# Output projection of attention computed feature-major and transposed back, its input passes one unit earlier

## The reference, cut to what matters

```python
h = _L0_tok_ref(x, ...)                                   # (16, 512, 128)
h = h + _L0_attn_ref(_layernorm(h), W_qkv, b_qkv, W_out, b_out)
h = h + _L0_ffn_ref(_layernorm(h), router_w, router_b, Wi, Wh, b, Wo, bo)
# at the end of _L0_attn_ref:
out = jnp.concatenate([out_wtok, out_fea], axis=1)
return out @ W_out + b_out
```

## Time and profile before

| | us |
|---|---|
| median of 3 runs | 1867.98 |
| lowest, highest | 1867.66, 1868.47 |
| the profiled execution | 1867.89 |
| its span, first to last instruction | 1866.0 |
| TensorE busy | 1740.3 |
| Vector busy | 1542.1 |
| ScalarE busy | 997.0 |

### The profile page before, as it was taken

The page is one execution under the profiler, slowest core; times in us unless marked ns, Lnnn a source line. Parts: engine busy times, 40 slices in busy tenths (PEclk is TensorE's granted clock), DMA queues, the critical chain, the costliest instruction groups (busy, mean ns, idle before and its releaser), DMA issues.

```text
span 1866.0 us, 25899 instructions
## 1 busy us (share of the span) xinstructions
PE 1740.3 (93%) x9898; PEld 852.3 (46%) x9898; DVE 1542.1 (83%) x2417; ACT 997.0 (53%) x1114; POOL 38.0 (2%) x42
## 2 busy tenths in 40 slices
PE   4447899999999999999999999999999999999998
PEld 2223444444444444544444444444444444444443
DVE  2649897988889888898988889898888988889865
ACT  4225645646465554646546464565646556464544
POOL 0000000000000000000000000000000000000000
PEclk9768999999999999999999999999999999999999
DMA  3123221313123131221323223131322314232121
GB/s 117 21 36 83 64 64 52 74 41 82 47 53 74 44 79 42 64 68 40 74 56 70 43 63 64 49 77 39 78 53 52 75 45 71 49 63 68 45 63 37
DMA packets 203905, 110.95 MB, mean 59 GB/s; under 512 B 125642, under 2 KB 184892, under 8 KB 203782
## 3 DMA queue, kind: packets, MB, share of 16 engines
q1 hardware_dynamic: 203782, 109.30, 25.8%
HBM read 89.84 MB, written 4.74 MB: 51 GB/s over the span
## 4 chain that ended last, share of the span: by engine, by line
PE 61%; DVE 26%; issue 7%; ACT 4%; DMA 1%; SPq 1%; POOL 0%; DVEq 0%; ACTq 0%
PE gates L528 45%; PE yp L534 4%; DVE tmp L1024 3%; DVE tmp L1003 2%; DVE xm L996 2%; DVE Hs L1008 2%; DVE C L1028 2%; DVE tmp L1018 2%; DVE tmp L1039 2%; ACT tmp L677 2%; PE FB L488 2%; PE FA L469 2%; PE FB L487 2%; PE FA L454 2%; DVE z L1043 1%
## 5 line engine op out<-in xcount | busy, mean ns | idle before, releaser
L670 ACT ACTIVATE tmp<-gates,bias_sb 128x1024 f32<-128x1024 f32 x504 | 559.7, 1111 | 571.4 <-PE gates L528 570.1
L528 PE MATMUL gates<-xm,wi_sb 128*128 128x512 f16 x3024 | 759.1, 389 | 14.2 <-DVE xm L996 9.5
L528 PE MATMUL gates<-Hs,wh_sb 128*128 128x512 f16 x2880 | 708.1, 382 | 0.0
L528 PEld LDWEIGHTS gates<-xm,wi_sb 128*128 128x128 f16 x3024 | 294.5, 100 | 410.9 <-issue 117.0
L528 PEld LDWEIGHTS gates<-Hs,wh_sb 128*128 128x128 f16 x2880 | 284.8, 99 | 349.1 <-issue 16.3
L677 ACT ACTIVATE tmp<-C 128x1024 f32<-128x1024 f32 x128 | 135.2, 1056 | 149.6 <-DVE C L1028 145.7
L1003 DVE SCALAR_TENSOR_TENSOR tmp<-tmp 128x1024 f32<-128x1024 f32 x128 | 156.5, 1223 | 58.6 <-ACT tmp L677 56.7
L1018 DVE SCALAR_TENSOR_TENSOR tmp<-tmp 128x1024 f32<-128x1024 f32 x120 | 145.2, 1210 | 64.3 <-ACT tmp L670 64.3
L1024 DVE SCALAR_TENSOR_TENSOR tmp<-tmp,C 128x1024 f32<-128x1024 f32 x120 | 145.7, 1214 | 39.4 <-ACT tmp L670 38.8
L996 DVE TENSOR_TENSOR xm<-xs,masks 128x2048 f16<-128x2048 f16 x128 | 155.7, 1217 | 11.8 <-DMA masks<-mask_scratch 11.8
L1008 DVE SCALAR_TENSOR_TENSOR Hs<-tmp,Hs 128x1024 f16<-128x1024 f32 x120 | 146.7, 1222 | 16.3 <-ACT Hs L681 16.3
(11 more groups left out here) (155 smaller groups left out, 1231.0 us busy)
## 6 DMA issues: line engine op xcount, KB each, us to landing
masks<-mask_scratch SPq DMA_DIRECT2D x128, 256.0 KB, 5.2
roww<-mw_scratch SPq DMA_DIRECT2D x128, 256.0 KB, 3.5
rowk<-mask_scratch SPq DMA_DIRECT2D x128, 128.0 KB, 2.9
diag<-pr SPq DMA_DIRECT2D x64, 112.0 KB, 3.2
diag<-vwin SPq DMA_DIRECT2D x64, 112.0 KB, 3.2
out_dram<-h SPq DMA_DIRECT2D x16, 256.0 KB, 2.2
C<-in_wi SPq DMA_DIRECT2D x1, 2048.0 KB, 10.4
C<-in_wh SPq DMA_DIRECT2D x1, 2048.0 KB, 15.1
```

What stands on the lines that cost most here:

```text
L528: last = mm(gates[:, slot, k * SEQ:(k + 1) * SEQ], w, v, start=(i < K), stop=(i >= len(seq) - K))
L670: A(tmp[:, gate_at(gate, e), :], gates[:, (n - 1) % 2, :], ACT.Tanh, bias=bias_sb[:, e, gate:gate + 1], scale=UNSCALE).then_inc(s_tanh, 1)
```

## The change

The projection is computed feature-major: `wout_sb` is the stationary operand, the whole of `attn` (512 columns) the moving one, and the result, features by tokens, lies in `FA[:, 1, :]`. ScalarE reads it, adds the bias (now one value per partition) and writes `xnT`; TensorE transposes the four tiles back into `FB`, where the token-major result lay before. The matmul is in unit 16 on TensorE, ScalarE's pass in unit 16, the transposes in unit 17. Vector's four passes L914 move from unit 16 to unit 15, behind f_part of unit 14. `ones1` and its memset go, and the bias is loaded as a column.

```diff
--- before.py
+++ after.py
@@ -54,12 +54,12 @@
 
 
     SP_AT = dict(ids=-8, qbd=1, vz=5, rows=25, wrow=28)
-    PE_AT = dict(emb=-5, xT=-2, qkv=-1, summary=2, window=4, feature=10, values=15, proj=17, x2T=20,
+    PE_AT = dict(emb=-5, xT=-2, qkv=-1, summary=2, window=4, feature=10, values=15, proj=16, projT=17, x2T=20,
                  logits=21, maskT=25)
-    ACT_AT = dict(h=-5, xT=-2, qkv=-1, split=0, summary=4, window=7, pr_hi=11, feature=12, x2T=20,
+    ACT_AT = dict(h=-5, xT=-2, qkv=-1, split=0, summary=4, window=7, pr_hi=11, feature=12, proj=16, x2T=20,
                   choice=22, maskT=25)
     DVE_AT = dict(onehot=-6, moments=-4, xn=-3, pw=0, q_lo=0, kv_lo=1, v_win=2, w_max=3, s_max=5, s_sub=6, w_sum=7,
-                  w_out=8, s_sum=9, s_norm=10, f_max=11, p_lo=12, p_T=13, f_sum=14, f_part=14, attn=16,
+                  w_out=8, s_sum=9, s_norm=10, f_max=11, p_lo=12, p_T=13, f_sum=14, f_part=14, attn=15,
                   moments2=18, xn2=19, x_lo=21, choice1=22, choice2=22, weights=23)
     EARLY = 8
     MASKS_AT = 26
@@ -148,8 +148,7 @@
         rw_sb = sb("rw_sb", [P, E])
         rb_sb = sb("rb_sb", [P, E])
         bo_sb = sb("bo_sb", [P, D])
-        bout_sb = sb("bout_sb", [1, D])
-        ones1 = sb("ones1", [1, P])
+        bout_sb = sb("bout_sb", [P, 1])
         ident = sb("ident", [P, P])
         identb = sb("identb", [P, P], bf16)
         hones = sb("hones", [P, P])
@@ -245,7 +244,7 @@
 
         names = """ids enc onehot emb hsb bnst bnag veps rstd xn xnTp xnT qp kp vp q k v qbd vwin vz
             pw sw mw dw ew rw iw ow owr ow_c pf sf mf df ef rf if_ uf S mS dS eS rS iS prT O of0 of1
-            khi vhi qhi qlo klo vlo pn phi plo cf attn proj h2 bnst2 bnag2 veps2 rstd2 xn2 x2p xhi x32 xlo lgp lg m1 eq1 ix1 im1 k1 l2 m2
+            khi vhi qhi qlo klo vlo pn phi plo cf attn projT projS proj h2 bnst2 bnag2 veps2 rstd2 xn2 x2p xhi x32 xlo lgp lg m1 eq1 ix1 im1 k1 l2 m2
             eq2 ix2 im2 k2 dd ed sd w0 w1 wa wb wt mwc mwp mrow wT mout wout ybo"""
         S = {n: sem("f_" + n) for n in names.split()}
 
@@ -279,10 +278,13 @@
         def row(ap):
             return ap.rearrange("(a n) -> a n", a=1)
 
+        def col(ap):
+            return ap.rearrange("(n a) -> n a", a=1)
+
         consts = [
             (wqkv_sb[:, :], w_qkv), (bqkv_sb[:, :], b_qkv), (wout_sb[:, :], w_out),
             (rw_sb[:, :], router_w), (rb_sb[:, :], row(router_b).to_broadcast([P, E])), (bo_sb[WT0:WT0 + E, :], bo),
-            (bout_sb[:, :], row(b_out)), (ident[:, :], ident_dram), (hones[:, :], head_ones), (band_sb[:, :], band),
+            (bout_sb[:, :], col(b_out)), (ident[:, :], ident_dram), (hones[:, :], head_ones), (band_sb[:, :], band),
             (par_sb[:, :], parity), (m8_sb[:, :], expert_m8), (vcol[:, :], vocab_col),
             (bias_sb[:, :, :], b_lstm),
             (rows[0:ENC0 + NFR, :], frame_rows), (table[0:ENC0 + NFR, :], emb_table),
@@ -483,9 +485,11 @@
                     last.then_inc(S["O"], 1)
                 if t == PE_AT["proj"]:
                     pe.wait_ge(S["attn"], b1)
+                    mm(FA[:, 1, :], wout_sb[:, :], attn[:, :], start=True, stop=True).then_inc(S["projT"], 1)
+                if t == PE_AT["projT"]:
+                    pe.wait_ge(S["projS"], b1)
                     for i in range(TILES):
-                        mm(FB[:, i * D:(i + 1) * D], attn[:, i * P:(i + 1) * P], wout_sb[:, :], start=True, stop=False)
-                        last = mm(FB[:, i * D:(i + 1) * D], ones1[:, :], bout_sb[:, :], start=False, stop=True)
+                        last = nc.tensor.transpose(FB[:, i * D:(i + 1) * D], xnT[:, i * P:(i + 1) * P], ident[:, :])
                     last.then_inc(S["proj"], 1)
                 if t == PE_AT["x2T"]:
                     pe.wait_ge(S["xn2"], b1)
@@ -564,7 +568,7 @@
 
             pe.wait_ge(s_const, 16 * len(consts))
             pe.wait_ge(s_zero, 1)
-            pe.wait_ge(s_prep, 4)
+            pe.wait_ge(s_prep, 3)
             for t in range(-EARLY, NG * E):
                 front(t, 0)
             pe.wait_ge(s_wlo, 7)
@@ -602,7 +606,7 @@
                     act.wait_ge(S["xnTp"], b1)
                     A(xnT[:, :], FB[:, :], ACT.Copy).then_inc(S["xnT"], 1)
                 if t == ACT_AT["qkv"]:
-                    act.wait_ge(s_prep, 4)
+                    act.wait_ge(s_prep, 3)
                     act.wait_ge(S["qp"], b1)
                     if not is_zero(b):
                         act.wait_ge(S["S"], b)
@@ -639,6 +643,9 @@
                 if t == ACT_AT["feature"]:
                     act.wait_ge(S["df"], b1)
                     A(ew[:, 0:TF], prod[:, 0:TF], ACT.Exp).then_inc(S["ef"], 1)
+                if t == ACT_AT["proj"]:
+                    act.wait_ge(S["projT"], b1)
+                    A(xnT[:, :], FA[:, 1, :], ACT.Identity, bias=bout_sb[:, 0:1]).then_inc(S["projS"], 1)
                 if t == ACT_AT["x2T"]:
                     act.wait_ge(S["x2p"], b1)
                     A(x32[:, :], FB[:, :], ACT.Copy).then_inc(S["x32"], 1)
@@ -746,7 +753,6 @@
                     dve.wait_ge(s_dft_hi, 1)
                     STT(out=dft16[:, LO, :], in0=dft_sb, scalar=V_SCALE, in1=dft16[:, HI, :],
                         op0=ALU.mult, op1=ALU.subtract).then_inc(s_dft_lo, 1)
-            V.memset(ones1[:, :], 1.0).then_inc(s_prep, 1)
             dve.wait_ge(s_const, 16 * len(consts))
             V.tensor_copy(identb[:, :], ident[:, :]).then_inc(s_prep, 1)
             V.tensor_copy(bandb[:, :], band_sb[:, :]).then_inc(s_prep, 1)
```

## The result

The changed kernel takes 1821.03 us (median of 4 runs, 1818.52 to 1822.79) against 1868.22 us beside it. The ratio is 0.9744, interval [0.9728, 0.9761]: faster by 2.6%. The profiled execution has a span of 1821.0 us, 45.0 less than before.

A forecast was written before the change was run, and what follows sets the result against it. TensorE, busy 109.55 of 110.90 us per step, was taken as the bound; fourteen steps gaining 3.1 us (43.6) plus 2 and 1.5 for the first two fronts, in all 47, took 1867.9 to 1821 us, range 1809 to 1833.

The forecast's parts named there:

- The moved wait: TensorE ahead of the projection in unit 16: wait on Vector's passes not removed, 1.7 us instead of 1.4.
- Projection and weight load: TensorE, unit 16: one 512-column float32 matmul, 0.86 us, plus 0.2 us for a weight load that waits with it.
- the case for 1818: Weight load ahead of the new matmul is pulled ahead and its 0.2 us vanish: sum 3 us better.
- Tanh 17 late: ScalarE's tanh 17 begins at 1053.1, behind the later gates 17; Vector waits 1.5 us for it ahead of L1018.
- Wait for xn2: TensorE ahead of L493, unit 20: a second new wait, 0.6 us, and 0.15 us of weight load.
- ScalarE's pass: 512-wide activation adding the bias, unit 16, ahead of tanh 17: 588 ns, costing nothing on the path.
- Per step: Gates 17 to L493 takes 15.21 us against 18.33: gain 3.1 us per step, 43.6 us over fourteen steps.
- The clock: Granted clock stays 0.99 or more in the steps, with no 36-gate row above 7.9.
- A: Rival: clock still falls once in each step, costing 20 to 24 us, about 1843 us; chance 0.14.
- B: Rival: clock falls behind each of two new waits, 5.1 us lost per step, 1892 us; chance 0.04.
- Why the clock had fallen: Around the old projection: TensorE's idle gap followed by 3.3 us of thin matmuls lowers the clock.
- The first two fronts: Ahead of the steps and in step 0: gains of 2 us and 1.5 us.

The follow-up runs named there:

- e1: The change with Vector's passes left in unit 16, wide projection in unit 17, transposes in unit 18; 1814.33 us, 0.9705 of the kernel before.
- e4: The kernel before, its thin projection moved to unit 16 and Vector's passes to unit 15; 1886.40 us, 1.0094 of the kernel before.
- e2: The kernel before, thin projection kept in unit 17, with only Vector's passes moved from unit 16 to 15; 1823.78 us, 0.9750 of the kernel before.
- e3: The change with its projection and ScalarE's pass in unit 17, transposes in unit 18; 1798.79 us, 0.9620 of the kernel before.
- The longer gap: The change with three more unread 512-column passes on Vector ahead of the passes into attn; 1858.37 us, 0.9942 of the kernel before.
- the later tail: On top of e3, all that follows xn2 one unit later, masks' transposes and rows included; 1787.22 us, 0.9560 of the kernel before.

## Why the prediction was right, and where it was not

The forecast was 1821 with the clock up and 3 to 4 us per step, and so it came. By its steps:

- *Bound and pace.* Right. TensorE stayed the engine that sets the step, and what Vector and it had to wait for each other moved to where the text put it.
- *The moved wait.* Forecast 1.66 us of it between y's stream and the end of the passes, 1.5 as the profile counts. Measured 1.56 (1025.60 to 1027.16), 1.45 as counted.
- *Projection and weight load.* Forecast 1.06 us. Measured 1.02 (1027.16 to 1028.18). The load did wait: it starts at 1027.21, behind the passes, as the row had it. The rule of the Trainium skill ("TensorE: Matmul & The Clock Gate", "Step-by-step: what each phase is for") is about loads pulled ahead of matmuls under way, and doesn't speak of a wait; the case for 1818 stretched it.
- *Tanh 17 late.* Forecast a hole of 1.5 us on Vector. Measured 1.48.
- *Wait for xn2.* Forecast 0.79 us from the end of y's stream to L497. Measured 0.54 (1039.84 to 1040.38).
- *ScalarE's pass.* 672 ns on average, not 588, and in the steps hidden as forecast: the transposes start right behind gates 17, at 1030.77.
- *Per step.* Forecast 3.1 us, measured 3.56 over the last thirteen distances (111.02 to 107.46). The miss is the sum of small terms, each a little dear.
- *The clock.* It stayed up, as forecast. What it was worth can be told now. Before, a step with a short slow stretch was 110.18 us from gates 17 to gates 17. From the start of its projection to L493 it took 13.58 us (1051.50 to 1065.08). The same instructions without a slow stretch are in the kernel with the move only:

```profile
921.29 0.38 PE L487 MATMUL FB<-wout_sb,attn 128*128 128x128 f32 x2
...
933.15 0.60 PE L493 MATMUL FB<-ident,xn 128*128 128x128 f32 x4
```

That is 11.86 us, to which 0.1 comes for the first weight load, laid bare by before's wait. So the short stretch cost 1.62, and 108.6 is left; the step with a long one gives the same (15.14 from 1161.69 to 1176.83, so 3.2 lost of 111.8). The prices of A and B for one stretch, 1.4 to 1.7 and 3.4, were near. Of the 3.56 us per step about 2.45 are then the clock, and 1.1 is the form less the dearer waits. The change wins mostly by what it does to the clock.

*Why the clock had fallen* was put too narrowly. I laid it to the gap together with the thin matmuls. That it is the wide form that holds the clock up, at gaps up to 1.45 us, is shown by three pairs of kernels that differ in the form alone: before and e1 have slow stretches in 14 steps and in none, e4 and the change in 11 and in none, e2 and e3 in 4 and in none. Over all of them the runs show: gap of 1.2 us and thin matmuls, 14 steps of 14; gap of 1.5 us and thin matmuls a unit earlier, 11; thin matmuls alone, 4; a gap of 3.25 us between wide matmuls, 7; a gap of 1.45 us between wide ones, none. Either can do it alone in some steps. Nearly all undisturbed steps of one kernel agree to some hundredths of a microsecond, so what picks one step and spares the next is not a difference in the work that these traces show. It stays open. The Trainium skill ("TensorE: Matmul & The Clock Gate", "HAM oscillation — how this bites in real kernels") lays it to idle gaps. The longer gap agrees with that; the four steps of e2, without a gap in the records, do not.

*The first two fronts* together came out with the wrong sign, and this is the term of the sum that failed. I gave them a gain of 3.5 us. In the first front, ahead of the steps, Vector waited 4.06 us instead of 5.95, a gain of 1.9 as forecast (2). But the pass of the third front, in step 1, begins later than before; here from the timelines of before and after:

```profile
245.80 0.63 DVE L861 TENSOR_TENSOR prod<-qT,oW 128x448 f32<-128x448 f32 x1
```

```profile
249.27 0.63 DVE L867 TENSOR_TENSOR prod<-qT,oW 128x448 f32<-128x448 f32 x1
```

That is 3.5 us lost by then. 0.9 of it is there from the start: the constants are in place at 16.93 us, not 16.02. In the two other kernels that keep the bias as a row they are there at 16.27 and 16.62, in those with the column at 16.50 to 17.06. These overlap, so that the column costs anything isn't shown. Most of the loss comes in two places of step 0, at 180 to 190 us and at 200 to 205 us, where ScalarE's tanh fall back by 2.4 and 2.2 us. The clock reads 0.50 there for 10.2 and 6.8 us (the first is shown above); before it did so only from 194.3 to 197.7. (From 153.3 to 173.7 it is the other way: the mean granted clock was 0.67 before, and is 0.83.) There TensorE has holes in every kernel of this study. The changed kernel had more to lose there than its shorter projection gained; that it must be so isn't shown, since the form-only kernel, with slow stretches in the same places, lost 1.9, and the one with the later tail lost 0.5 (its pass is at 246.28), though its mean clock from 130 to 210 us, 0.81, is below the change's 0.83. What sets the clock in step 0, and what it costs there, stays open.

The sum then: 13 distances of 3.56 are 46.3 us, the last stretch is 2.1 shorter, the beginning 3.5 longer: 45.0. The forecast of 47 was 43.6 and 3.5. The exact hit on 1821 is luck in part: two misses of 5 and 7 us all but cancel, and the 2 us left are within the scatter of the four runs, of which the profiled one, 1822.79, was the longest.

## What to carry to other kernels

Before moving work ahead to end a wait, look whether the instruction that waits moves with it: here the passes came a unit earlier, the projection too, and the wait stayed; leaving the projection where it was gained 1.57 us per step more. When an engine is nearly full, read the granted clock around its few thin or idle places: here it was worth 2.45 of 3.56 us per step, and in the kernel before one number of a table was enough to keep it up in ten steps of fourteen. And after such a change look for the one who is late next (here xn2): moving what hangs on it by one unit gained another 0.74 us per step.

## What the runs showed of the hardware

- Sixteen narrow float32 instructions (eight matmuls of 128 columns) took 3.33 us at full clock behind a wait and 3.23 without one; one matmul of 512 columns took 0.96 and 0.86, and four transposes 0.44.
- The clock can fall behind a stretch of narrow matmuls in which the profile shows no idle time of TensorE (3.60 of 3.60 us busy); it did in 4 steps of 14.
- GpSimd's power on 128x4 numbers took 1.01 us in every step before, and in the changed kernel 1.91 where Vector's L1030 and L1034 run beside it at once instead of waiting. It ended just in time and cost nothing here. The kernel with the move only shows both within one kernel: 2.02 to 2.04 us in its ten steps without a slow stretch, where Vector's L1024 runs beside it, and 1.01 in the four others, where L1024 comes later. These are its lines in one step of each kind:

```profile
928.53 2.02 POOL L1115 TENSOR_TENSOR rstd<-veps,mhalf 128x4 f32<-128x4 f32 x1 [75.49 <-DVE veps L933]
...
1035.61 1.01 POOL L1115 TENSOR_TENSOR rstd<-veps,mhalf 128x4 f32<-128x4 f32 x1 [75.50 <-DVE veps L933]
```

So it goes with Vector's passes beside it; by what way they hold it up is not shown.
